# Attention inside a two-layer kernel: the order of the steps worked out by a list schedule, and the copy of each finished block moved to ScalarE

## What is computed

```
Qh, Kh, Vh = heads of relu(x @ W + b)
scores = einsum('bqhd,bkhd->bhqk', Qh, Kh) / sqrt(dh)
scores = NEG where the key is masked or lies after the query
attn = softmax(scores, axis=-1) * query_mask
out  = einsum('bhqk,bkhd->bqhd', attn, Vh)          # then + x, norm, gamma, beta
```

## Time and profile before

| what | value |
|---|---|
| median of 3 runs | 2173.13 us (2168.01 to 2175.15) |
| profiled execution, its own time | 2178.65 us |
| span of that execution | 2176.2 us |
| granted TensorE clock, mean | 0.940 |
| attention, first to last matmul | about 295.9 to 1254.6 us |
| in that, a middle stretch of 760 us (420 to 1180): PE, DVE, ACT busy | 710.6, 637.6, 506.9 us |

### The profile page before, as it was taken

How to read it: one execution, slowest core, us unless ns; L and a number is a source line. 1 busy time by engine, 2 the same in 40 slices (tenths; PEclk the granted TensorE clock), 3 DMA queues, 4 the chain that set the end, 5 groups by cost and what they waited for, 6 DMA issues and landing times. The chain is left out here.

```text
span 2176.2 us, 34165 instructions
## 1 busy us (share of the span) xinstructions
PE 1814.4 (83%) x11999; PEld 944.1 (43%) x11999; DVE 1514.0 (70%) x3496; ACT 1031.5 (47%) x1908; POOL 536.8 (25%) x592
## 2 busy tenths in 40 slices
PE   0898926899999999999899959799327788999998
PEld 0565602222222222222223236555317555888865
DVE  7987656888888888888788845378206896444456
ACT  3554403466667666666566825356001444323210
POOL 1443350000000000000340000100650786566620
PEclk9999958999999999999999989999658899999999
DMA  3466563013030404040620163000420622566556
GB/s 97 140 212 220 187 157 69 1 25 127 12 140 3 148 2 150 2 150 2 227 79 11 40 230 128 18 2 1 158 85 9 214 95 94 175 188 187 185 198 222
DMA packets 158712, 238.67 MB, mean 110 GB/s; under 512 B 19762, under 2 KB 127282, under 8 KB 156882
## 3 DMA queue, kind: packets, MB, share of 16 engines
q1 hardware_dynamic: 122706, 152.46, 23.0%
q0 software_dynamic: 23136, 75.65, 9.5%
q10 hardware_dynamic: 12704, 8.39, 1.2%
HBM read 116.23 MB, written 119.82 MB: 108 GB/s over the span
## 5 line engine op out<-in xcount | busy, mean ns | idle before, releaser
L1051 ACT ACTIVATE c_prob<-c_pst 128x512 f32<-128x512 f32 (+1 forms) x1152 | 603.1, 573 | 362.3 <-PE c_pst L1012 221.5
L1159 DVE TENSOR_REDUCE c_mx<-c_pf 128x2 f32<-128x1024 f32 x384 | 463.0, 1223 | 92.3 <-PE c_pf L993 89.4
L1012 PE MATMUL c_pst<-c_qa,c_ka 128*128 128x512 bf16 (+3 forms) x1280 | 393.9, 358 | 38.2 <-DMA c_qa<-c_mT 34.6
L993 PE MATMUL c_pf<-c_ka,c_qa 64*128 64x512 bf16 (+3 forms) x1280 | 234.9, 364 | 79.2 <-DVE c_mx L1159 26.4
L1028 PE MATMUL c_po<-c_prob,c_vh 128*32 128x512 f32 (+3 forms) x2560 | 297.2, 547 | 1.5 <-DVE c_osb L1187 0.5
L1155 DVE CUSTOM_DVE_ANT_0 c_spare<-c_pf,c_cut 128x384 f32<-128x384 f32 (+3 forms) x512 | 231.1, 492 | 51.0 <-PE c_pf L993 46.3
L1012 PEld LDWEIGHTS c_pst<-c_qa,c_ka 128*128 128x128 bf16 x1280 | 108.6, 97 | 284.4 <-ACT c_prob L1051 122.7
L993 PEld LDWEIGHTS c_pf<-c_ka,c_qa 64*128 64x128 bf16 x1280 | 61.9, 93 | 313.0 <-issue 126.5
L925 POOL IOTA c_zero<- 128x24 int32 x6 | 1.3, 215 | 697.4 <-PE c_po L1028 697.4
L1980 POOL DMA_INDIRECT s_parts<-x_yr,x_tags x144 | 141.0, 979 | 85.8 <-DVE x_yr L2635 62.4
L2519 PE MATMUL x_ps<-x_gu,x_xs 128*128 x576 | 137.6, 382 | 0.0
(11 more groups left out here) (383 smaller groups left out, 2934.9 us busy)
## 6 DMA issues: line engine op xcount, KB each, us to landing
s_slots<-c_zero POOLq DMA_DIRECT2D x6, 3264.0 KB, 19.9
x_xr<-s_slots SPq DMA_DIRECT2D x72, 272.0 KB
x_rows<-s_parts SPq DMA_DIRECT2D x8, 2048.0 KB, 8.8
c_qa<-s_qs SPq DMA_DIRECT2D x64, 192.0 KB, 8.3
c_ka<-s_ks SPq DMA_DIRECT2D x64, 192.0 KB, 9.0
s_qs<-b_parts SPq DMA_DIRECT2D x32, 256.0 KB, 2.4
s_ks<-b_parts SPq DMA_DIRECT2D x32, 256.0 KB, 2.7
s_vs<-b_va SPq DMA_DIRECT2D x32, 256.0 KB, 3.8
```

The costliest lines, as they stand in the source:

```text
L993: mm = nc.tensor.matmul(pf[:, slot, h - fh, 0:kn], qa[r, s, h, qt * P:(qt + 1) * P], ka[r, s, h, k0:k0 + kn], start=True, stop=True, tile_ ...
L1012: mm = nc.tensor.matmul(pst[:, u % NS, at:at + qn], ka[:, s, hh, kt * P:(kt + 1) * P], qa[:, s, hh, qb * QB + q0:qb * QB + q0 + qn], start ...
L1051: nc.scalar.activation(prob[:, g % NP, hh, 0:w], pst[:, u % NS, 0:w], ACT.Exp).then_inc(exp_ok, 1)
L1159: nc.vector.tensor_reduce(mx[:, fh:fh + 2, qt, part], pf[:, slot, :, 0:kn], AX.X, ALU.max).then_inc(max_ok, 1)
```

## The change

The fixed pattern gives way to a list schedule. `plan()` keeps estimated times of PE, ACT and DVE, of the `c_pst`, `c_pf` and `c_prob` buffers, and of the arrival of the rows (7.5 us behind DVE's copy). At each turn it lists the kinds of step that could come next with the time at which each could start (0.1 us later when it is of another kind than the step before, 0.06 us behind its input), and takes the one with the least start less a fixed preference. Scores may be up to NP = 3 groups ahead of values. The lead of the firsts grows from 0.34 to 0.67 of a unit. The take directly follows its values in the list, as before, but ACT carries it out. No instruction is added or dropped otherwise, and no buffer changes.

```diff
-    LAG, NP = 2, 3
+    NP, SLOTS = 3, 2
...
+    SWITCH, SIGNAL, DRAIN, ROW = 0.1, 0.06, 0.17, 1 / 2400
+    prefer = dict(first=0.11, score=0.0, values=-0.18, rows=0.17, turn=0.29)
 
     def lead(s):
-        return min(0.52, 0.21 + 0.6 * s)
+        return min(0.67, 0.34 + 0.51 * s)
...
+        def start(kind, ready):
+            return max(pe + (SWITCH if kind != shape else 0.0), ready + SIGNAL)
...
+        def score_ready():
+            j, hh = divmod(scores, HQ)
+            n, g = divmod(j, NG)
+            if j - values >= NP or (n, groups[g][0]) not in rows_at:
+                return None
+            ready = exp_end[scores - NS] if scores >= NS else 0.0
+            return max(ready, rows_at[n, groups[g][0]]) if hh == 0 and g in opens else ready
+
+        def values_ready():
+            if (values + 1) * HQ > scores or values % NG in last and turns:
+                return None
+            ready = exp_end[(values + 1) * HQ - 1]
+            return max(ready, taken[-1]) if values % NG in opens else ready
+
+        while values < NQ * NG:
+            ready = {"score": score_ready() if scores < NQ * NG * HQ else None, "values": values_ready()}
+            if firsts < NQ * N1 and firsts // N1 <= values // NG + 1 and spent + share1[firsts % N1] / 2 <= passed + lead(passed):
+                ready["first"] = slot_free[-SLOTS]
+            if split_:
+                ready["rows"] = max(split_[0][0], slot_free[-SLOTS])
+            if turns:
+                ready["turn"] = max(turns[0][0], slot_free[-SLOTS])
+            ready = {kind: at for kind, at in ready.items() if at is not None}
...
+            kind = min(ready, key=lambda k: start(k, ready[k]) - prefer[k])
...
+                slot_free.append(reduce_at(end + DRAIN + 0.043, 1.14 * kn / W1 if whole else 2 * (0.153 + 0.00104 * kn) + 0.02))
...
+                rows_at[m, qb] = dve + 7.5
...
+                slot_free.append(reduce_at(issue(kind, at, 0.24) + DRAIN, 1.15))
...
+                act = max(act, end) + 0.065 + 0.00084 * width[g]
+                exp_end.append(act + 0.1)
...
+                values_end.append(issue(kind, at, 4 * width[g] * ROW) + DRAIN)
...
+                    act = max(act, values_end[-1] + SIGNAL) + 0.55
...
         @block.scalar
         def _(act):
             for kind, n, g, hh in steps:
+                if kind == "take":
+                    act.wait_ge(values_ok, n * NG + (last[g] + 1))
+
+                    wait(act, turn_ok, n * NB + g)
+                    nc.scalar.copy(osb[:], po[:]).then_inc(take_ok, 1)
...
-                elif kind == "take":
-                    dve.wait_ge(values_ok, n * NG + (last[a] + 1))
-
-                    wait(dve, turn_ok, n * NB + a)
-                    nc.vector.tensor_copy(osb[:], po[:]).then_inc(take_ok, 1)
```

More of the change, by code:

```diff
@@ L708, in attention, with issue, reduce_at @@
     last = [max(g for g in range(NG) if groups[g][0] == qb) for qb in range(NB)]
-    LAG, NP = 2, 3
+    NP, SLOTS = 3, 2
     assert NG % NP == 0
-    cost1 = [f[3] + 64 for f in first]
-    width = [sum(p[2] for p in g[1]) + 64 for g in groups]
+    share1 = [(f[3] + 64) / sum(f[3] + 64 for f in first) for f in first]
+    width = [sum(p[2] for p in g[1]) for g in groups]
+    share2 = [(w + 64) / sum(w + 64 for w in width) / HQ for w in width]
     done_at = [max(i for i, f in enumerate(first) if f[1] // 4 == qb) for qb in range(NB)]
+    opens = [g for g in range(NG) if g == 0 or groups[g - 1][0] != groups[g][0]]
+    SWITCH, SIGNAL, DRAIN, ROW = 0.1, 0.06, 0.17, 1 / 2400
+    prefer = dict(first=0.11, score=0.0, values=-0.18, rows=0.17, turn=0.29)
     def lead(s):
-        return min(0.52, 0.21 + 0.6 * s)
+        return min(0.67, 0.34 + 0.51 * s)
     def plan():
-        steps, done, spent, passed, chain_, waiting = [], 0, 0.0, 0.0, [], []
+        steps, chain_, split_, turns = [], [], [], []
+        exp_end, values_end, slot_free, rows_at, taken = [], [], [0.0] * SLOTS, {}, [0.0]
+        pe, shape, act, dve = 0.0, None, 0.0, 0.0
+        firsts = scores = values = 0
+        spent = passed = 0.0
+        def start(kind, ready):
+            return max(pe + (SWITCH if kind != shape else 0.0), ready + SIGNAL)
+        def issue(kind, ready, stream):
+            nonlocal pe, shape
+            begun = start(kind, ready)
+            pe, shape = begun + stream, kind
+            return pe
+        def reduce_at(ready, cost):
+            nonlocal dve
+            dve = max(dve, ready) + cost
+            return dve
         def chain_step():
@@ L729, in chain_step @@
                 steps.append(("max", m, qb, k))
+                ready = reduce_at(0.0, 0.19)
                 if k == 5:
[L731 to L736, removed]
-                steps.append(("first", m, i, 0))
-                spent += cost1[i] / sum(cost1)
-                done += 1
+                    split_.append((ready, m, qb))
@@ new lines, in plan @@
+        while values < NQ * NG:
[7 more added lines that the diff above has]
+            ready = {kind: at for kind, at in ready.items() if at is not None}
+            if not ready:
+                if chain_:
+                    chain_step()
+                    continue
+                ready["first"] = slot_free[-SLOTS]
+            kind = min(ready, key=lambda k: start(k, ready[k]) - prefer[k])
+            at = ready[kind]
+            if kind == "first":
+                m, i = divmod(firsts, N1)
+                fh, qt, k0, kn, part = first[i]
+                steps.append(("first", m, i, 0))
+                end = issue(kind, at, kn * ROW)
+                whole = k0 + kn < (qt + 1) * P
+                slot_free.append(reduce_at(end + DRAIN + 0.043, 1.14 * kn / W1 if whole else 2 * (0.153 + 0.00104 * kn) + 0.02))
+                firsts += 1
+                spent += share1[i]
@@ L744, in first_steps @@
                     chain_step()
[L746 to L754, removed]
-                    chain_step()
[L756 to L767, removed]
@@ L768, in plan @@
-        assert done == NQ * N1 and not waiting and not chain_
+            elif kind == "rows":
+                ready_, m, qb = split_.pop(0)
+                steps.append(("rows", m, qb, 0))
+                slot_free.append(reduce_at(issue(kind, at, SIGNAL) + DRAIN, 0.2))
+                rows_at[m, qb] = dve + 7.5
+            elif kind == "turn":
+                ready_, n, a = turns.pop(0)
+                steps.append(("turn", n, a, 0))
+                slot_free.append(reduce_at(issue(kind, at, 0.24) + DRAIN, 1.15))
+            elif kind == "score":
+                if firsts == NQ * N1:
+                    chain_step()
+                j, hh = divmod(scores, HQ)
+                n, g = divmod(j, NG)
+                qb, pieces = groups[g]
+                steps.append(("score", n, g, hh))
+                end = issue(kind, at, width[g] * ROW + sum(0.063 if p[0] >= 4 * qb else 0.008 for p in pieces)) + DRAIN + 0.037
+                if hh == 0 and j >= NP:
+                    end = max(end, values_end[j - NP] + SIGNAL)
+                act = max(act, end) + 0.065 + 0.00084 * width[g]
+                exp_end.append(act + 0.1)
+                scores += 1
+                passed += share2[g]
+            else:
+                n, g = divmod(values, NG)
+                steps.append(("values", n, g, 0))
+                values_end.append(issue(kind, at, 4 * width[g] * ROW) + DRAIN)
+                values += 1
+                if g in last:
+                    a = last.index(g)
+                    steps.append(("take", n, a, 0))
+                    act = max(act, values_end[-1] + SIGNAL) + 0.55
+                    taken.append(act + 0.1)
+                    turns.append((taken[-1], n, a))
@@ L769, in plan @@
+        steps.extend(("turn", n, a, 0) for ready_, n, a in turns)
+        assert firsts == NQ * N1 and not chain_ and not split_
         return steps
```

## The result

The kernel after takes 2089.99 us (median of 4 runs, 2082.73 to 2091.80), the one before 2170.57 (4 runs beside it, 2167.47 to 2175.15). The ratio is 0.9621, 95% interval 0.959 to 0.9652: 81 us less, of which 63 were forecast. The profiled execution took 2091.8 us, its span is 2090.1. Attention, from first to last matmul, went from 958.7 us (295.9 to 1254.6) to 876.8 (295.5 to 1172.3), 81.9 us less. The other 4 us of the spans' difference of 86.1 lie behind attention, in code that did not change. Unit by unit, from last turn to last turn, unit 0 gave back 28 us (it ends at 457.3, before at 485.3), the six behind it 4 to 12 us each and the last one 8.

A forecast was written before the change was run, and what follows sets the result against it. PE's order, with its waits and changes of shape, was taken to set the pace; 28 + 25 + 13 + 4 - 2 - 5 = 63 us off the 2173.13 us median gave 2110, with an 8-in-10 range of 2070 to 2155.

The forecast's parts named there:

- one part at a bound: Whole kernel: the forecast's own range with one term at its bound, given as 2083 to 2133 us.
- part 3: PE's order: 0.4 fewer changes of shape a group over 288 groups, 13 us gained; bounds 32 gained, 5 lost.
- part 2: PE's firsts: put where DVE has freed a slot, 25 of 41.4 us of waits gained; bounds 0 and 41.
- What bounds it: PE's order: Attention: PE's order sets the pace, 106 us a unit without waits against 111 measured.
- Part 1: PE's scores: rows no longer waited for, 28 of 34.6 us gained; bounds 20 and 34.6.
- Part 4: Behind the last first: some 19 groups gain 0.2 us each, 4 us; bounds 6 gained, 5 lost.
- Part 5: The 32 takes on ACT at 0.587 us each: hidden by ACT's idle time, except 2 us charged in the last stretch.
- Part 6: Whole list: 5 us charged for new waits where its durations are wrong; bounds 0 and 15.
- Rival D: ACT: uncovered takes block exponentials, then scores, by 1.9 us each, 61 us in all; 2209 us, chance 0.07.
- B: PE and DVE: waits only change place, only the rows are gained, 25 us; 2148 us, chance 0.18.
- C: All of attention: nearly everything is gained, 107 us; 2066 us, chance 0.10.

The follow-up runs named there:

- run 5: Kernel before, with a first put ahead of one score at 92 places, giving 92 fewer changes of shape: 2160.27 us, ratio 0.9957 to before.
- run 7: Kernel after with each of the 512 mask products issued twice, 28 us more work on PE alone: 2111.23 us, ratio 0.9717 to before.
- run 8: Kernel before with each mask product issued twice, 28 us more work on PE: 2187.8 us, ratio 1.0077 to before.
- run 1: Kernel before with only the copy of each block moved from DVE to ACT: 2167.06 us, ratio 0.9968 to before.
- run 2: Kernel after with the copy back on DVE, its plan still reckoning with ACT: 2106.49 us, ratio 0.9691 to before.
- run 4: Kernel before with the cap of its firsts' lead raised from 0.52 to 0.67 unit: 2186.29 us, ratio 1.0058 to before.
- run 3: Kernel after with the lead of before (0.21 to 0.52 unit): 2137.19 us, ratio 0.9837 to before.
- run 6: Kernel after, its plan taking rows as there with DVE's copy, not 7.5 us later: 2101.66 us, ratio 0.9691 to before.
- run 12: Kernel after with its own durations but other preferences and lead 0.31 to 0.65, on another chip: 2054.94 us, ratio 0.9675 to before there.
- run 10: Kernel after with the preference of firsts at 0 for 0.11, on another chip: 2113.66 us, ratio 0.9965 to before there.
- run 9: Kernel after with a masked reduction's fixed time in the plan 0.076 for 0.153 us, on another chip: 2042.03 us, ratio 0.9617 to before there.

## Why the prediction was right, step by step

The direction and, in the main, the mechanisms held, and the time lies in the range. The forecast gain was 63 us and the measured one 81. The terms for waits were close in sum, and the one for changes of shape was half of what came. The range for "one part at a bound" was added up wrong: by the terms' own bounds it is 2091 (part 3 at 32) to 2135 (part 2 at 0), not 2083 to 2133, so that the measured 2090 lies at its very end; it is the wider range, to 2070, that holds it.

- **What bounds it: PE's order.** Held. Runs 5, 7 and 8 show that time on PE is on the path, and run 1 that DVE's 22 us alone buy 7. But "DVE's load is slack" holds for before only: after, both count (runs 2 and 7).
- **Part 1, rows, 28 us.** The wait fell by 34.6 - 2.7 = 31.9. The reason I gave was half right. 21.8 us of it were three waits in unit 0 and 12.3 those of block 2 behind the load, as I read them. Block 3, for which I worked out 11 us of notice against 27, was waited for only once, 0.5 us. I put the middle waits down to the lead alone; run 4 shows that the lead in the old order only moves them to slots, and run 3 that the list without it has 38.2 us of waits for rows. It takes both, and the plan's 7.5 us as well (run 6).
- **Part 2, slots, 25 us.** Firsts: 41.4 to 11.8, so 29.6 gained; 9.9 us are new at rows and turns. Before had 2.5 us of that kind, PE lines 999 and 1037 together. Net about 22. That the copy would help this was written, with no number of its own; run 2 gives 15 us for it.
- **Part 3, changes of shape, 13 us.** Mis-sized: I took 0.4 fewer a group, it was 226 / 288 = 0.78, so 25 us. Of the 226, 181 are runs of scores (779 before, 598 after): the list lets two or three scores pass in one piece, where I had the present pattern less one piece in some groups.
- **Part 4, the end, 4 us.** Behind the last first stand the scores of 24.0 groups (18.75 before), and they and what follows take 57.4 us (48.9 before): 2.39 us a group for 2.61. At 0.21 for 18.75 groups that is 4 us, as forecast. The 24 groups held as well; the 2.2 us a group that I named for them did not, if the last values are counted in. The timeline shows three scores, not four, in a piece, and none waits. That uses up the scores' lead over the values, and further on longer pieces follow:

```profile
1157.53 1.06 PE L1096 MATMUL c_po<-c_prob,c_vh 128*32 128x512 f32 x8
1158.53 0.82 PE L1080 MATMUL c_pst<-c_qa,c_ka 128*128 128x512 bf16 x3
1159.28 1.06 PE L1096 MATMUL c_po<-c_prob,c_vh 128*32 128x512 f32 x8
```

- **Part 5, the take on ACT.** The duration held, a median of 587 ns as in the row it was taken from the earlier trace rows, and in mid-stage no idle time of ACT stands before it. The groups of ACT from 420 to 1100:

```profile
L1124 ACT ACTIVATE c_prob<-c_pst 128x512 f32<-128x512 f32 (+1 forms) x931 | 471.1, 580 | 199.2 <-PE c_pst L1080 122.6 <-PE c_pst L1084 74.3
L1115 ACT COPY c_osb<-c_po 128x512 f32<-128x512 f32 x26 | 15.5, 597 | 0.0
```

  Over all 32 it waited 8.9 us, in four places. Rival D does not occur.
- **Part 6, misfit, 5 us.** The 9.9 us at rows and turns are of this kind, and are set off in part 2. Parts 1 to 4 as measured come to 83 us, where attention lost 82; part 4 is made of waits and changes that the others count in part, so this split is a rough one.
- **Rivals.** B ("the waits only change place") is what run 4 shows for the old order, not for the list. C, with all terms at their bounds, was nearest in part 3. Most of what I had named for the profile came so: the wait for rows under 10 us, a unit of 104 us, DVE at 89%, a copy of 0.59 us.

## What to carry to other kernels

Where three engines are each 70 to 95% busy and wait for one another in turn, ask what PE's fixed order makes it stand before, and price a change of matmul shape with the waits: here 0.10 to 0.11 us each, 226 of them worth some 23 us beside 59 of waits. A deeper lead is no gain by itself; it pays only where the order can use it, and here it had to bring block 2's rows ahead of the load in SP's order, with the DMA's time in the plan. A list schedule is as good as its model: one that left out the DMA's time lost 15 us (run 6), and this one leaves out that SP issues in order, so it rated run 12's list better than after's, and it was slower. Fewer changes of shape at any price (run 10) lost nearly all of the gain.

## What the runs showed of the hardware that was not expected

Products on another shape of the array cost about 0.11 us at each change, 0.145 behind the 32-column values, and the same in all fourteen traces; run 5 shows it in the whole time. Other operands alone don't cost it: a mask product of 128 columns and the score behind it, of one shape, start 0.05 us apart, which is the time of the columns. A busy share of 105 in 111 us did not mean that PE was full, since a unit now takes 104; the earlier trace rows shows why, as its two scores start 0.21 us apart and each is drawn 0.39 long. The kernel before took 2171 to 2173 us on the chips of the first runs and 2119 on that of the last four. Attention is about as long there (878.4 us in run 9, 876.8 in after); behind it run 9 is 53 us shorter, nearly all of it in one later stage. No trace shows one list on both chips, and the cause is open.
